# Attention kernel on one core: two value products behind the next block's scores, maxima rows first in each score group, denominators split 3 and 1

## The chip, the cores and the metric

The kernel runs on one core of a Trainium2 chip. The metric is device time in microseconds (us), from the first to the last instruction of one execution. Engines are named as in the profile: PE is TensorE's matmuls, PEld its weight loads, DVE is VectorE, ACT is ScalarE, POOL is GpSimd, SP is SyncE, which issues most transfers.

## The reference, cut to what matters

Sixteen images of 128 channels and 32 x 32 pixels go through a convolution-style attention, then a second, linear attention over tokens, then a mixture of experts. The change touches the first attention alone. It has 4 heads of 32 channels over 1024 pixels, so each image has four 1024 x 1024 score matrices.

```python
qkv = jnp.einsum('oc,bchw->bohw', qkv_w, xn) + qkv_b[:, None, None]
q, k, v = (qkv[:, :, :hd], qkv[:, :, hd:2 * hd], qkv[:, :, 2 * hd:])
attn = jnp.einsum('bnchw,bncyx->bnhwyx', q, k) / jnp.sqrt(jnp.float32(C))
attn = jax.nn.softmax(attn.reshape(B, n, H, W, H * W), axis=-1)
av = jnp.einsum('bnhwyx,bncyx->bnchw', attn, v).reshape(B, C, H, W)
out = jnp.einsum('oc,bchw->bohw', out_w, av) + out_b[:, None, None]
```

## The kernel before, in words

The program is written out per engine and runs as a software pipeline. One iteration belongs to one image for its softmax attention, and holds later stages of the images before it and early stages of the image after it. An iteration is cut into 32 quarters `q`, four to a step: `s, j = divmod(q, 4)`. Every engine walks through the same quarters in its own queue, and semaphores alone tie the queues together.

A block is 128 keys against 512 queries (half an image) for all four heads. An image has 16 blocks, two in each step: their scores stand on PE at j = 0 and j = 2. In what follows a **score group** is the eight products of `scores`: four of q and k, one per head, with 32 rows of contraction each (L1755), then four of the "maxima rows" with 2 rows of contraction in bf16 (L1758). The latter subtract each query's maximum, so that the exponential stays in range. The four heads' products go to four banks of PSUM (the matmul output memory), and the four stand in different row strips of the array, so they run side by side. ACT then takes the exponential of a block in two halves (L928), and PE may write the next score group only when both are done (the wait on `exp_done`). A **values group** is the four products of `values` (L1789) that multiply one block's probabilities with v. They lie side by side in column strips.

The maxima have to be known before the exponential. PE therefore computes the scores of the image or half that comes later a second time with bf16 operands, one **row tile** of 128 queries x 512 keys at a time (L1814), and DVE reduces each to its maxima (L1345). The row tiles alternate between two PSUM banks (`row_ps`). A quarter has two of them, `row_tile(0)` and `row_tile(1)`, and each waits until DVE has read the tile two before it:

```python
ps = row_ps[kh]
pe.wait_ge(row_used, n - 1)
```

Between the two row tiles of a quarter stand the **pieces**: products of the other stages (projections L1602, L1609, L1627; transposes; the rank of tokens L1664 to L1668; the Gram matrix L1639), set to quarters by the table `AT`. Pieces and softmax denominators share one PSUM bank, and `free_shared` waits until it has been drained. The denominators (L1736) sum the probabilities over keys. POOL first adds the blocks of a pair (L729), four pairs to a half, and `DEN_STEPS` says which pairs' products stand in which of two quarters that follow each other.

Of the kernel before, what the change touches and what calls it, by code (L numbers as in the profile page):

```python
# [19 lines left out]
def conv_attention_hybrid_kernel(  # L20
# [25 lines left out]
    NH = 4  # L46
    HD = C // NH
# [4 lines left out]
    E, _, HID = L1_ffn_W1.shape  # L52
# [30 lines left out]
    out_v = out.rearrange("b c h w -> b c (h w)")  # L83


    AT = {'q0': 2, 'k0': 3, 'q1': 4, 'k1': 7, 'rank': 1, 't2_0': 8, 't2_1': 10, 'proj0': 11, 'proj1': 12, 'mrow1': 14, 'v0': 13, 'v1': 16, 'z2T0': 17, 'z2T1': 18, 'logits': 20, 'zT0': 23, 'zT1': 27, 'mrow0': 29, 'gram': 28, 'usum': 30, 'xn': 0, 'values1': 0, 'values0': 17, 'x_bias': 27, 'ln1': 11, 'z2': (12, 14, 14, 15), 'gexp': 21, 'ln0': 16, 'z': (18, 18, 20, 21), 'square': 21, 'ln_heads': 26, 'split': (2, 3, 5, 6), 'norm1': 5, 'norm0': 29, 'd16': (20, 20), 'u': (22, 23), 'scatter': (8, 10, 11, 13, 16, 17, 22, 24), 'max1': 12, 'max0': 28, 'kv1': 2, 'kv2': 4, 'kv3': 5, 'slot_numbers': 4, 'stats1a': 8, 'stats1b': 10, 'deviations1': 11, 'gate': (20, 21, 23, 23, 24, 25, 25, 25, 26, 26, 26, 27, 27, 27, 27, 27), 'prefix': (27, 28, 30), 'stats0a': 11, 'stats0b': 12, 'deviations0': 17, 'gsum': (19, 20), 'ss': (22, 24), 'heads': 26, 'turn': 1, 'den_sum': 2, 'sum': (5, 9, 13, 19), 'den1': 5, 'den0': 21}

    LAG = {
# [16 lines left out]
    def table(pair, p):  # L105

        return AT if 2 * pair + p < B else AFTER[2 * pair + p - B]

# [7 lines left out]
    def in_range(lag, pair, p):  # L116

        return 0 <= 2 * pair + p + lag < (B if lag > -3 else ROUTED)

    def image(lag, pair, p):  # L120

        return 2 * (pair + (p + lag) // 2) + (p + lag) % 2, pair + (p + lag) // 2, (p + lag) % 2
# [8 lines left out]
    def at_quarter(q, pair, p):  # L131

        return [n for n in order(pair, p) if table(pair, p)[n] == q and in_range(LAG[n], pair, p)]
# [6 lines left out]
    def positive(value):  # L140

        return not isinstance(value, int) or value > 0
# [9 lines left out]
    def row_target(r):  # L152

        return (0, 1, r) if r < 4 else (1, 0, r - 4) if r < 8 else (1, 1, 0)

    def denominators_at(pair, p):

        return tuple((table(pair, p)[n], LAG[n], int(n[3])) for n in order(pair, p) if n[:3] == "den")

    DEN_STEPS = ((0, (0, 1)), (1, (2, 3)))  # L160

    def ring_slots(n):

        slots = list(range(NKB))
        for _ in range(n):
            slots = slots[1::2] + slots[0::2]
        return slots
# [7 lines left out]
    def startup_rows(b, half):  # L175

        return b == 0 and half == 0
# [10 lines left out]
    def steps_before(s, n):  # L188

        return (0, s - n) if s >= n else (-1, STEPS + s - n)  # L190
# [38 lines left out]
    with ctx:  # L229
        def sb(name, shape, dt=F32):  # L230
            return ctx.enter_context(nc.sbuf_tensor(name, shape, dt))
# [44 lines left out]
        ones_b = sb("ones_b", [P, P], BF16)  # L276
# [3 lines left out]
        xn = sb("xn", [P, N])  # L280
        part = sb("part", [P, 2, 2, N], BF16)
        qk = sb("qk", [P, 2, 2, N])
# [7 lines left out]
        mrow = sb("mrow", [P, 2, HALF], BF16)  # L290
# [13 lines left out]
        z = sb("z", [P, BLK, C])  # L304
        gsum = sb("gsum", [P, 2, BLK * NG])
        d16 = sb("d16", [P, BLK, C])
        ss16 = sb("ss16", [P, 7, BLK * NG])
        rs16 = sb("rs16", [P, 2, BLK * NG])
        u = sb("u", [P, BLK, C + 1])
        usum = sb("usum_sb", [P, 1])  # L310
# [66 lines left out]
        row_ps, st_ps, av_ps, shared_ps = bank[0:2], bank[2:6], bank[6], bank[7]  # L377
# [1191 lines left out]
        def _(pe):  # L1569
            t_ = nc.tensor  # L1570
# [171 lines left out]
            def scores(b, par, s, j):  # L1742

                half, kb = s // 4, 2 * (s % 4) + j // 2
                keys = slice(kb * P, (kb + 1) * P)
                queries = slice(half * HALF, (half + 1) * HALF)
                if kb == 0:
                    pe.wait_ge(mrow_ready, 2 * b + half + 1)
                    if half == 0:
                        pe.wait_ge(raw_ready, 4 * b + 4)  # L1750
                if positive(32 * b + 4 * s + j):
                    pe.wait_ge(exp_done, 32 * b + 4 * s + j)
                for h in range(NH):
                    rows_ = slice(HD * h, HD * h + HD)
                    t_.matmul(st_ps[h], qk[rows_, par, 1, keys], qk[rows_, par, 0, queries], start=True, stop=False)  # L1755
                for h in range(NH):
                    rows_ = slice(HD * h, HD * h + 2)
                    last = t_.matmul(st_ps[h], ones_b[rows_, :], mrow[rows_, half, :], start=False, stop=True)  # L1758
                    if h % 2 == 1:
                        last.then_inc(st_ready, 1)  # L1760

# [14 lines left out]
            def values(b, par, sv, g):  # L1776

                half = sv // 4
                kb = 2 * (sv % 4) + g
                pe.wait_ge(exp_done, 32 * b + 4 * sv + 2 * g + 2)  # L1780
                if kb == 0:

                    if positive(2 * b + half):
                        pe.wait_ge(av_out, 2 * b + half)
                    pe.wait_ge(v_ready, 2 * b + 2)
                group = prob_groups[ring_slots(2 * b + half)[kb]]
                for h in range(NH):
                    rows_ = slice(HD * h, HD * h + HD)
                    mm = t_.matmul(av_ps[rows_, :], v_sb[:, par, kb, rows_], group[:, h, :],  # L1789
                                   start=(kb == 0), stop=(kb == NKB - 1))  # L1790
                if g == 1:
                    mm.then_inc(probs_used, 1)

            def iteration(pair, p):
                at = table(pair, p)
                for q in range(QUARTERS):
                    s, j = divmod(q, 4)
                    if 2 * pair + p == FIRST and q == OTHER_WEIGHTS_AT:
                        other_weights()

                    def row_tile(kh):
                        lag, half, h = row_target(s + 1)
                        if not in_range(lag, pair, p):
                            return
                        b, pr, par = image(lag, pair, p)
                        if startup_rows(b, half):
                            return
                        if half == (1 if b == 0 else 0) and j == 0 and kh == 0:
                            pe.wait_ge(stacked1[par][h], 16 * STACK1_DMAS * (pr + 1))
                        n = 64 * b + 32 * half + 8 * h + 2 * j + kh  # L1810
                        ps = row_ps[kh]
                        pe.wait_ge(row_used, n - 1)
                        qb = 4 * half + j
                        t_.matmul(ps[:, :], qs1[:, par, h, qb * P:(qb + 1) * P],  # L1814
                                  ks1[:, par, h, kh * HALF:(kh + 1) * HALF], start=True, stop=True)\
                          .then_inc(row_ready, 1)

                    for first, u in FIRST_ROWS:
                        if 2 * pair + p == FIRST and q == first:
                            first_rows(u)  # L1820
                    if j % 2 == 1:
                        lag, sv = (steps_before(s, 1) if j == 1 else (0, s))
                        if in_range(lag, pair, p):
                            b, _, par = image(lag, pair, p)
                            values(b, par, sv, 1 if j == 1 else 0)
                    for first, lag, half in denominators_at(pair, p):
                        for later, pairs in DEN_STEPS:
                            if q == first + later and in_range(lag, pair, p):
                                if later == 0:
                                    free_shared(f"den{half}", pair, p)  # L1830
                                denominators(image(lag, pair, p)[0], half, pairs)
                    if j % 2 == 0 and in_range(0, pair, p):
                        b, _, par = image(0, pair, p)
                        scores(b, par, s, j)
                    row_tile(0)
                    for name in at_quarter(q, pair, p):
                        if name[:3] != "den":
                            piece(name, pair, p)
                    row_tile(1)
                    for t in steps_at(q, pair, p):  # L1840
                        step(t)
# [171 lines left out]
```

## Time and profile before

| what | value |
| --- | --- |
| median of 3 runs | 1842.6 us (1842.03, 1842.6, 1848.09) |
| profiled execution | span 1848.0 us, near the third of these runs |
| PE, PEld | 1707.3 us busy (92%), 842.7 us (46%) |
| DVE, ACT, POOL | 1338.6 us (72%), 1140.8 us (62%), 1279.6 us (69%) |
| softmax stage | from 52.6 us (first exponential) to 1377.6 us (end of the last) |

Read it by stages. The change acts in the softmax stage only, which is 16 iterations long; the experts behind it keep their instructions. In that stage the shares of the engines differ from those of the whole span, so they are taken from a window of their own. PE's busy time includes the overlap of pipelined products, and so the start of one product and the start of the next are read rather than durations.

### The profile page before, as it was taken

To read this page: it belongs to the slowest core of one execution; us is meant where nothing else is said; L and a number is where in the kernel's file an instruction comes from. 1 tells how busy PE (TensorE), PEld (TensorE's weight loads), DVE (VectorE), ACT (ScalarE), POOL (GpSimd) and SP (SyncE) were. 2 spreads that over 40 slices of the span, in tenths; PEclk is the share of its full clock that TensorE was granted. 3 is DMA by queue.
4 is the path that set the end of the run, shared out by engine and by line. 5 is a ranking of instruction groups with operands and counts; after the bars stand their busy time and mean duration, and the time that the engine had idled before them with its cause. 6 is when DMAs were issued, how large, how long until landed. Compare 5 with 4: busy or idle time off the path is not lost. (4 is left out here: it accounts for less than half of the span.)

```text
span 1848.0 us, 36083 instructions
## 1 busy us (share of the span) xinstructions
PE 1707.3 (92%) x11741; PEld 842.7 (46%) x11741; DVE 1338.6 (72%) x3555; ACT 1140.8 (62%) x2019; POOL 1279.6 (69%) x1165
## 2 busy tenths in 40 slices
PE   5999989999999999999999999999976889999999
PEld 2223333333434333333334343333335778888776
DVE  5567788888878888888878888878755555555474
ACT  2556565666656665666666566656544777777553
POOL 1466747787878778787778787787874767777500
PEclk8899999999999999999999999999997889999998
DMA  2302112130303031230303030312212334454394
GB/s 77 91 13 58 35 47 61 46 90 29 88 19 88 19 92 46 65 85 23 92 27 89 19 89 18 92 37 63 67 58 78 92 95 127 156 173 137 102 288 157
DMA packets 119206, 144.43 MB, mean 78 GB/s; under 512 B 18248, under 2 KB 83044, under 8 KB 119024
## 3 DMA queue, kind: packets, MB, share of 16 engines
q1 hardware_dynamic: 103856, 110.91, 21.4%
q0 software_dynamic: 14784, 31.23, 5.0%
q8 instruction: 97, 1.59, 0.4%
q14 instruction: 85, 0.70, 0.1%
q10 hardware_dynamic: 384, 0.00, 0.0%
HBM read 59.38 MB, written 50.05 MB: 59 GB/s over the span
## 5 line engine op out<-in xcount | busy, mean ns | idle before, releaser
L1345 DVE TENSOR_REDUCE rowmax<-psum 128x1 f32<-128x512 f32 x992 | 652.3, 682 | 210.0 <-PE psum L1814 203.9
L1814 PE MATMUL psum<-arena 128*128 128x512 bf16 x992 | 360.4, 390 | 38.2 <-DVE rowmax L1345 35.7
L928 ACT ACTIVATE arena<-psum 128x1024 f32<-128x1024 f32 x256 | 253.9, 1022 | 161.1 <-PE psum L1758 161.1
L928 ACT ACTIVATE probs<-psum 128x1024 f32<-128x1024 f32 x256 | 253.1, 1020 | 114.5 <-PE psum L1758 114.2
L1755 PE MATMUL psum<-qk 32*128 32x512 f32 x2048 | 293.9, 643 | 10.0 <-ACT probs L928 4.6
L1814 PEld LDWEIGHTS psum<-arena 128*128 128x128 bf16 x992 | 88.5, 99 | 448.0 <-DVE rowmax L1345 333.4
L715 POOL DMA_INDIRECT sorted_scratch<-rows,slot_idx x224 | 220.3, 984 | 96.8 <-issue 51.9
L729 POOL TENSOR_TENSOR probs<-probs 128x512 f32<-128x512 f32 x172 | 218.9, 1273 | 27.2 <-PE psum L1789 16.1
L729 POOL TENSOR_TENSOR arena<-arena 128x512 f32<-128x512 f32 x172 | 218.9, 1272 | 22.0 <-PE psum L1789 10.1
L803 POOL DMA_INDIRECT y_scratch<-xn,d_tile x120 | 116.9, 974 | 57.5 <-issue 28.7
L1865 PE MATMUL psum<-qk 128*128 128x256 f32 x476 | 129.5, 396 | 20.0 <-ACT qk L988 18.9
L803 POOL DMA_INDIRECT y_scratch<-qk,d_tile x118 | 115.0, 974 | 45.9 <-issue 26.0
L706 POOL TENSOR_TENSOR part<-qk,part 128x512 bf16<-128x512 f32 x64 | 74.0, 1157 | 94.3 <-ACT qk L848 90.7
L1789 PE MATMUL psum<-arena,v_sb 128*32 128x512 f32 x1024 | 138.5, 613 | 0.0
L1789 PE MATMUL psum<-probs,v_sb 128*32 128x512 f32 x1024 | 136.4, 605 | 0.0
L1755 PEld LDWEIGHTS psum<-qk 32*128 32x128 f32 x2048 | 80.5, 183 | 120.5 <-issue 78.3
L1882 PEld LDWEIGHTS psum<-arena,x_in 128*128 128x128 f32 x952 | 128.0, 198 | 13.8 <-issue 7.5
L1882 PE MATMUL psum<-arena,x_in 128*128 x952 | 130.9, 282 | 3.1 <-ACT x_in L1000 3.1
L1000 ACT ACTIVATE x_in<-psum,b_tile 128x256 f32<-128x256 f32 x238 | 100.0, 472 | 38.4 <-issue 31.8
L729 POOL TENSOR_TENSOR arena<-arena,probs 128x512 f32<-128x512 f32 x80 | 102.1, 1277 | 12.9 <-PE psum L1789 7.6
L729 POOL TENSOR_TENSOR probs<-probs,arena 128x512 f32<-128x512 f32 x80 | 102.0, 1275 | 5.5
L1758 PE MATMUL psum<-mrow,ones_b 2*128 2x512 bf16 x1024 | 102.0, 378 | 0.0
(256 smaller groups left out, 2876.5 us busy)
## 6 DMA issues: line engine op xcount, KB each, us to landing
arena<-part SPq DMA_DIRECT2D x256, 128.0 KB, 3.1
part<-sorted_scratch SPq DMA_DIRECT2D x119, 144.0 KB
x_in<-in_x_dram SPq DMA_DIRECT2D x16, 512.0 KB, 3.2
x_res<-in_x_dram SPq DMA_DIRECT2D x16, 512.0 KB, 5.7
t_scratch<-t SPq DMA_DIRECT2D x14, 512.0 KB, 6.4
arena<-t_scratch SPq DMA_DIRECT2D x10, 512.0 KB
probs<-y_scratch SPq DMA_DIRECT2D x16, 256.0 KB, 4.2
out_dram<-v_sb SPq DMA_DIRECT2D x16, 256.0 KB, 3.9
```

The lines of the kernel that those rows point to most:

```text
L715: g.indirect_dma_start(out=sorted_dram, out_offset=bass.IndirectOffsetOnAxis(ap=slot_idx[:, par, n:n + 1], axis=0), in_=rows[:, par, n % B ...
L729: piece = g.tensor_tensor(even[:, cols], even[:, cols], odd[:, cols], ALU.add)
L803: g.indirect_dma_start(out=y_dram, out_offset=bass.IndirectOffsetOnAxis(ap=d_tile[:, i, k:k + 1], axis=0), in_=y_out[i][:, k, :], in_offse ...
L928: a.activation(group[:, 2 * i:2 * i + 2, :].rearrange("p s n -> p (s n)"), st_pair[i], ACT.Exp, scale=float(C) ** -0.5).then_inc(exp_done, 1)
L1000: a.activation(hid[t % 2][:, j, :], bank[t % 2][:, j * TILE:(j + 1) * TILE], ACT.Gelu, bias=b1_tile[:, t % 2, j:j + 1]).then_inc(hid_ready, 1)
L1345: v.tensor_reduce(rowmax[:, half, kh, h, j:j + 1], row_ps[kh][:, :], AX.X, ALU.max)\
L1755: t_.matmul(st_ps[h], qk[rows_, par, 1, keys], qk[rows_, par, 0, queries], start=True, stop=False)
L1758: last = t_.matmul(st_ps[h], ones_b[rows_, :], mrow[rows_, half, :], start=False, stop=True)
L1789: mm = t_.matmul(av_ps[rows_, :], v_sb[:, par, kb, rows_], group[:, h, :], start=(kb == 0), stop=(kb == NKB - 1))
L1814: t_.matmul(ps[:, :], qs1[:, par, h, qb * P:(qb + 1) * P], ks1[:, par, h, kh * HALF:(kh + 1) * HALF], start=True, stop=True)\
L1865: last = t_.matmul(bank[t % 2][:, j * TILE:(j + 1) * TILE], w1_tile[t % 2][:, j * P:(j + 1) * P], zT_tile[t % 2], start=True, stop=True)
L1882: last = t_.matmul(bank[4 + t % 2][:, k * P:(k + 1) * P], hid[t % 2][:, j, k * P:(k + 1) * P], w2[:, bass.ds(e, 1), j, :].rearrange("p a c ...
```

## The change

Three things are done. The two values groups of a step, which stood at j = 1 and j = 3 (each between the row tiles of two quarters), now both stand at j = 0 straight behind the score group, and they take the two blocks of the step before. In a score group the maxima rows go first and open the accumulation, and the products of q and k close it, so that the semaphore for ACT now hangs on these. The denominators' pairs go three and one instead of two and two, and stand behind the scores of their quarter. ACT's evacuation of the values of the first half moves one quarter up (`values0`).

```diff
-'values0': 17
+'values0': 16
...
-    DEN_STEPS = ((0, (0, 1)), (1, (2, 3)))
+    DEN_STEPS = ((0, (0, 1, 2)), (1, (3,)))
...
                 for h in range(NH):
+                    rows_ = slice(HD * h, HD * h + 2)
+                    t_.matmul(st_ps[h], ones_b[rows_, :], mrow[rows_, half, :], start=True, stop=False)
+                for h in range(NH):
                     rows_ = slice(HD * h, HD * h + HD)
-                    t_.matmul(st_ps[h], qk[rows_, par, 1, keys], qk[rows_, par, 0, queries], start=True, stop=False)
-                for h in range(NH):
-                    rows_ = slice(HD * h, HD * h + 2)
-                    last = t_.matmul(st_ps[h], ones_b[rows_, :], mrow[rows_, half, :], start=False, stop=True)
+                    last = t_.matmul(st_ps[h], qk[rows_, par, 1, keys], qk[rows_, par, 0, queries], start=False, stop=True)
                     if h % 2 == 1:
                         last.then_inc(st_ready, 1)
...
-                    if j % 2 == 1:
-                        lag, sv = (steps_before(s, 1) if j == 1 else (0, s))
+                    if j % 2 == 0 and in_range(0, pair, p):
+                        b, _, par = image(0, pair, p)
+                        scores(b, par, s, j)
+                    if j == 0:
+                        lag, sv = steps_before(s, 1)
                         if in_range(lag, pair, p):
                             b, _, par = image(lag, pair, p)
-                            values(b, par, sv, 1 if j == 1 else 0)
+                            values(b, par, sv, 0)
+                            values(b, par, sv, 1)
...
-                    if j % 2 == 0 and in_range(0, pair, p):
-                        b, _, par = image(0, pair, p)
-                        scores(b, par, s, j)
```

The next two fences show PE's order in the first step of an iteration, from the score group at q = 0 on: L1755 and L1758 are the score group, L1814 the row tiles, L1789 the values, L1664 to L1668 the rank. First before:

```order
L1755 MATMUL psum<-qk 128x512 x4
L1758 MATMUL psum<-mrow,ones_b 128x512 x4
L1814 MATMUL psum<-arena 128x512 x2
L1789 MATMUL psum<-arena,v_sb 32x512 x4
L1814 MATMUL psum<-arena 128x512
L1664 MATMUL psum<-chosen,tri 128x64
L1666 MATMUL psum<-before,ones 128x64
L1668 MATMUL psum<-before,ones 128x8
L1814 MATMUL psum<-arena 128x512
```

And in the changed kernel, at the same place:

```order
L1755 MATMUL psum<-mrow,ones_b 128x512 x4
L1758 MATMUL psum<-qk 128x512 x4
L1789 MATMUL psum<-probs,v_sb 32x512 x4
L1789 MATMUL psum<-arena,v_sb 32x512 x4
L1814 MATMUL psum<-arena 128x512 x3
L1664 MATMUL psum<-chosen,tri 128x64
L1666 MATMUL psum<-before,ones 128x64
L1668 MATMUL psum<-before,ones 128x8
L1814 MATMUL psum<-arena 128x512
```

Two values groups now stand ahead of the first row tile of the step, and between the step's row tiles none is left; the line numbers 1755 and 1758 have changed their products. The second place is the denominators of an image's second half, at q = 5 and 6 of the following iteration; L1602 is the projection to q that stands at q = 4, L1736 the denominators. Before, again on PE:

```order
L1755 MATMUL psum<-qk 128x512 x4
L1758 MATMUL psum<-mrow,ones_b 128x512 x4
L1814 MATMUL psum<-arena 128x512
L1602 MATMUL psum<-xn,wqkvT 128x512
L1814 MATMUL psum<-arena 128x512
L1789 MATMUL psum<-probs,v_sb 32x512 x4
L1736 MATMUL psum<-probs,ones 32x512 x8
L1814 MATMUL psum<-arena 128x512 x2
L1736 MATMUL psum<-probs,ones 32x512 x8
L1755 MATMUL psum<-qk 128x512 x4
```

And changed:

```order
L1755 MATMUL psum<-mrow,ones_b 128x512 x4
L1758 MATMUL psum<-qk 128x512 x4
L1789 MATMUL psum<-arena,v_sb 32x512 x8
L1814 MATMUL psum<-arena 128x512
L1602 MATMUL psum<-xn,wqkvT 128x512
L1814 MATMUL psum<-arena 128x512
L1736 MATMUL psum<-probs,ones 32x512 x12
L1814 MATMUL psum<-arena 128x512 x2
L1755 MATMUL psum<-mrow,ones_b 128x512 x4
L1758 MATMUL psum<-qk 128x512 x4
L1736 MATMUL psum<-probs,ones 32x512 x4
```

The values group that stood between L1602 and the first denominators has gone ahead of L1602, three pairs stand together, and the fourth comes behind the next score group. On DVE and SP nothing moves; on ACT the evacuation L911 goes ahead of two small operations.

## Rows read from the trace of the kernel before

**Rows 1.** Busy time of each engine in the softmax stage (count of instructions in brackets).

```profile
52.60:1377.60 1325.00, 1252.76 (x8954) 477.40 (x8953) 1051.82 (x2443) 836.24 (x1252) 1016.59 (x863) 0.98 0.20 57
```

**Rows 2.** Groups of instructions: busy us, mean ns; idle time before them, what ended it.

```profile
L1345 DVE TENSOR_REDUCE rowmax<-psum 128x1 f32<-128x512 f32 x992 | 652.3, 682 | 210.0 <-PE psum L1814 203.9
L1814 PE MATMUL psum<-arena 128*128 128x512 bf16 x992 | 360.4, 390 | 38.2 <-DVE rowmax L1345 35.7
```

**Rows 3.** Timeline of PE, first step of an image: start, duration (us), instruction.

```profile
622.46 1.14 PE L1755 MATMUL psum<-qk 32*128 32x512 f32 x8
623.42 0.40 PE L1758 MATMUL psum<-mrow,ones_b 2*128 2x512 bf16 x4
623.75 0.64 PE L1814 MATMUL psum<-arena 128*128 128x512 bf16 x2
624.32 1.07 PE L1789 MATMUL psum<-probs,v_sb 128*32 128x512 f32 x8
625.32 0.39 PE L1814 MATMUL psum<-arena 128*128 128x512 bf16 x1
...
626.13 0.38 PE L1814 MATMUL psum<-arena 128*128 128x512 bf16 x1
626.44 1.14 PE L1755 MATMUL psum<-qk 32*128 32x512 f32 x8
...
627.73 0.39 PE L1814 MATMUL psum<-arena 128*128 128x512 bf16 x1
...
631.67 1.14 PE L1755 MATMUL psum<-qk 32*128 32x512 f32 x8
```

**Rows 4.** Timeline of PE, second step of the same image, with the denominators.

```profile
633.19 1.02 PE L1602 MATMUL psum<-xn,wqkvT 128*128 128x512 f32 x2
...
635.56 1.06 PE L1736 MATMUL psum<-arena,ones 128*32 128x512 f32 x8
...
637.42 0.60 PE L1814 MATMUL psum<-arena 128*128 128x512 bf16 x2
...
639.81 1.14 PE L1755 MATMUL psum<-qk 32*128 32x512 f32 x8
...
642.63 0.39 PE L1814 MATMUL psum<-arena 128*128 128x512 bf16 x1
642.99 1.10 PE L1602 MATMUL psum<-xn,wqkvT 128*128 128x512 f32 x2
643.92 0.38 PE L1814 MATMUL psum<-arena 128*128 128x512 bf16 x1
644.23 1.14 PE L1755 MATMUL psum<-qk 32*128 32x512 f32 x8
```

**Rows 5.** Timeline of DVE in that first step.

```profile
624.18 1.29 DVE L1345 TENSOR_REDUCE rowmax<-psum 128x1 f32<-128x512 f32 x2 [0.23 <-PE psum L1814]
```

**Rows 6.** Timeline of all engines in a later step: a row tile that waits.

```profile
770.34 0.39 PE L1814 MATMUL psum<-arena 128*128 128x512 bf16 x1
...
770.60 0.65 DVE L1345 TENSOR_REDUCE rowmax<-psum 128x1 f32<-128x512 f32 x1
...
771.31 0.39 PE L1814 MATMUL psum<-arena 128*128 128x512 bf16 x1 [0.58 <-DVE rowmax L1345]
```

**Rows 7.** Timeline of ACT in the first and second step.

```profile
627.89 1.02 ACT L928 ACTIVATE probs<-psum 128x1024 f32<-128x1024 f32 x1 [0.43 <-PE psum L1758]
629.02 0.69 ACT L846 ACTIVATE part<-psum,bqk 128x512 bf16<-128x512 f32 x1
...
630.17 1.02 ACT L928 ACTIVATE probs<-psum 128x1024 f32<-128x1024 f32 x1
...
634.25 0.69 ACT L846 ACTIVATE part<-psum,bqk 128x512 bf16<-128x512 f32 x1
634.83 0.68 ACT L848 ACTIVATE qk<-psum,bqk 128x512 f32<-128x512 f32 x1
```

**Rows 8.** Group of the Gram products, in the same columns as rows 2.

```profile
L1639 PE MATMUL psum<-u 128*128 128x129 f32 x256 | 47.4, 361 | 20.3 <-POOL u L787 20.3
```

More of the change, by code:

```diff
@@ L83, in conv_attention_hybrid_kernel @@
     out_v = out.rearrange("b c h w -> b c (h w)")
-    AT = {'q0': 2, 'k0': 3, 'q1': 4, 'k1': 7, 'rank': 1, 't2_0': 8, 't2_1': 10, 'proj0': 11, 'proj1': 12, 'mrow1': 14, 'v0': 13, 'v1': 16, 'z2T0': 17, 'z2T1': 18, 'logits': 20, 'zT0': 23, 'zT1': 27, 'mrow0': 29, 'gram': 28, 'usum': 30, 'xn': 0, 'values1': 0, 'values0': 17, 'x_bias': 27, 'ln1': 11, 'z2': (12, 14, 14, 15), 'gexp': 21, 'ln0': 16, 'z': (18, 18, 20, 21), 'square': 21, 'ln_heads': 26, 'split': (2, 3, 5, 6), 'norm1': 5, 'norm0': 29, 'd16': (20, 20), 'u': (22, 23), 'scatter': (8, 10, 11, 13, 16, 17, 22, 24), 'max1': 12, 'max0': 28, 'kv1': 2, 'kv2': 4, 'kv3': 5, 'slot_numbers': 4, 'stats1a': 8, 'stats1b': 10, 'deviations1': 11, 'gate': (20, 21, 23, 23, 24, 25, 25, 25, 26, 26, 26, 27, 27, 27, 27, 27), 'prefix': (27, 28, 30), 'stats0a': 11, 'stats0b': 12, 'deviations0': 17, 'gsum': (19, 20), 'ss': (22, 24), 'heads': 26, 'turn': 1, 'den_sum': 2, 'sum': (5, 9, 13, 19), 'den1': 5, 'den0': 21}
+    AT = {'q0': 2, 'k0': 3, 'q1': 4, 'k1': 7, 'rank': 1, 't2_0': 8, 't2_1': 10, 'proj0': 11, 'proj1': 12, 'mrow1': 14, 'v0': 13, 'v1': 16, 'z2T0': 17, 'z2T1': 18, 'logits': 20, 'zT0': 23, 'zT1': 27, 'mrow0': 29, 'gram': 28, 'usum': 30, 'xn': 0, 'values1': 0, 'values0': 16, 'x_bias': 27, 'ln1': 11, 'z2': (12, 14, 14, 15), 'gexp': 21, 'ln0': 16, 'z': (18, 18, 20, 21), 'square': 21, 'ln_heads': 26, 'split': (2, 3, 5, 6), 'norm1': 5, 'norm0': 29, 'd16': (20, 20), 'u': (22, 23), 'scatter': (8, 10, 11, 13, 16, 17, 22, 24), 'max1': 12, 'max0': 28, 'kv1': 2, 'kv2': 4, 'kv3': 5, 'slot_numbers': 4, 'stats1a': 8, 'stats1b': 10, 'deviations1': 11, 'gate': (20, 21, 23, 23, 24, 25, 25, 25, 26, 26, 26, 27, 27, 27, 27, 27), 'prefix': (27, 28, 30), 'stats0a': 11, 'stats0b': 12, 'deviations0': 17, 'gsum': (19, 20), 'ss': (22, 24), 'heads': 26, 'turn': 1, 'den_sum': 2, 'sum': (5, 9, 13, 19), 'den1': 5, 'den0': 21}
     LAG = {
```

## The prediction

> **What bounds the kernel now.** I read the windows by stage first. In the softmax stage (1325 us of the 1848.0) PE is busy 1252.76 us, 95%, DVE 1051.82 (79%), POOL 77% and ACT 63% [rows 1]. So PE looks like the bound. The groups of instructions then show with whom it is interlocked: the 992 row tiles of PE and the 992 maxima of DVE are the pair with the most waiting between them. DVE waits 203.9 us for row tiles, PE itself only 35.7 us for maxima [rows 2]. Third I read the timeline of one image, to see how these waits are kept small: in the step of [rows 3] no two row tiles start more than 1.60 us apart (626.13 and 627.73), and two of them last DVE 1.29 [rows 5].
>
> The timeline gives every price needed, as the distance from one start to the next [rows 3]. A score group lasts 0.96 to its maxima rows and 0.33 from there to the next row tile: 1.29. A values group lasts 625.32 - 624.32 = 1.00. From a row tile to a group in strips it is 626.44 - 626.13 = 0.31; from a row tile to the next it is 0.22 (two last 0.60, one 0.38) [rows 4]. Hence each entry into strips costs 0.09. A step without pieces is 2 x (1.29 + 1.00 + 2 x 0.22 + 2 x 0.31) = 6.70 us of PE; the mean of 128 steps (16 images of 8) is 1325 / 128 = 10.35, and the other 3.65 are pieces, denominators and waits.
>
> **The change, part by part.**
>
> *Maxima rows first.* The same eight products. The two passes of a score product then end the group. A values group has the same two passes and exit, 1.00, and a pass of 512 columns is 0.22, so I take 1.22 for the group. Bounds: 1.29 (nothing gained), and 1.08 if it also loses its exit as the second of two groups in strips does (0.86 + 0.22). Gain 0.07 per group.
>
> *Two values groups together.* Two pairs of denominators, products of the same shape, last 637.42 - 635.56 = 1.86 [rows 4], so the second group adds 0.86 rather than 1.00. The entry falls away twice in a step. PE saves 2 x 0.07 + 0.14 + 2 x 0.09 = 0.46 us a step.
>
> *What the values groups leave behind.* A row tile may start only when DVE has read the tile two before it. DVE starts a maximum 0.43 us after its tile (623.75 and 624.18), takes 0.68, and follows with the next after 1.29 - 0.68 = 0.61 [rows 2, 3, 5]; the waiting tile starts 0.06 after the maximum's end (771.31 against 770.60 + 0.65) [rows 6]. So behind an idle DVE the third tile comes no sooner than 0.43 + 0.68 + 0.06 = 1.17 after the first, and the fourth 0.61 later. Before, a values group (0.31 + 1.00) lies exactly between the second and third tile and hides this. Afterwards it stands ahead of the first tile, where DVE has its two last tiles to read (1.29) and PE brings nothing for 1.22 + 1.86 + 0.31 = 3.39.
>
> The first step, worked from its score group at 0 [rows 3]. Values to 3.08, first tile there; DVE 3.51 to 4.19; third tile 4.25; the rank between third and fourth takes 626.13 - 625.32 = 0.81, fourth tile 5.06; next score group 5.37. Before it was 626.44 - 622.46 = 3.98: 1.39 longer. The second half of the step loses its values group, but the next score group needs the exponentials. ACT ends the second at 630.17 + 1.02 = 631.19, which is 4.75 after the score group, with two copies of a projection between the two exponentials [rows 7]. This chain shortens by the 0.07 only, and a release takes 0.05, so the half lasts 4.73 against 631.67 - 626.44 = 5.23: 0.50 shorter. The step is 0.89 longer. With no piece and no exponential in the way the halves would be 5.17 and 3.31, 1.78 more than 6.70; with full cover by pieces the step would be 0.46 shorter. I take 0.87 for the five steps of this kind (first, third, fourth, fifth, seventh), by the one that I worked.
>
> *Denominators 3 and 1.* Their count stays. In the second step the first of them wait for ACT's two copies of L1602's projection: they start at 635.56, 0.05 after 634.83 + 0.68 [rows 4, 7], which is 2.37 behind L1602. Afterwards L1602 starts at 3.30 (values, tile, 0.22), the denominators at 5.67; three pairs 1.86 + 0.86, two tiles 0.53, next scores at 8.92. Before: 639.81 - 631.67 = 8.14. In the second half: scores and one pair to 2.22, third tile 3.39, then 644.23 - 642.63 = 1.60 as before: 4.99 against 4.42. The step is 1.35 longer. In the sixth step another piece stands there; without its wait the step would be 1.13 shorter than that, +0.2; I take 0.5. POOL's sums are asked for no sooner in the last pair, which stays a quarter behind; its cover is the two row tiles and the score group ahead of it.
>
> *The Gram step.* In the eighth step PE waits for POOL ahead of the Gram products, 20.3 us over 16 images [rows 8]. The second values group in front hides in this 1.27, the second half is shorter by 0.50 as above: -0.5.
>
> *Free.* The evacuation of values a quarter earlier on ACT follows exponentials that end later than the values do; if that cover is gone it delays ACT by at most the values' 1.86 once in an image. That PE asks POOL for sums sooner costs nothing while POOL has 23% idle.
>
> Sum per image: 5 x 0.87 + 1.35 + 0.5 - 0.5 = 5.7. Fifteen images have the row tiles of a following one throughout (the last I count at nothing): 85 us. Against the profiled 1848.0 that is 1933; that execution lies 5.4 over the median, so 1928.
>
> **The rivals.** *PE is the bound and simply has less to do* (faster). 128 x 0.46 = 59: 1784. For it: PE's 95%, and that PE's waits for DVE are so few. Against it: they are few because something always stands between the tiles. It decides if the waits at the third tile and for exponentials come to less than 0.46 us a step, that is if pieces stand there in most steps.
> The skill speaks for this rival: the Trainium skill, "TensorEngine Tiling (Array Packing)", Key Properties, says that changing the tiling mode drains TensorE. The trace agrees, with the 0.09 at each entry; by that rule alone the time would be the 1784 above.
>
> *Exponentials alone hold it.* DVE's waits are covered by pieces, and only the second halves cannot shrink below ACT's chain. First halves grow by 0.86 - 0.07 - 0.09 = 0.70, second ones fall by 0.50: 0.20 a step, 120 steps: 24, so 1867. For it: rows 7 hold in any case. Against: in the step worked, DVE's term is the larger.
>
> *It cancels* (no change). DVE's other work is about (1051.82 - 652.3) / 15 = 27 us an image; if half of it moves into the new gaps, tiles behind it come sooner, and the 5.7 goes to nothing: 1843. Against: DVE's queue is in order, and jobs that stand behind a maximum cannot go ahead of it.
>
> **How the numbers follow.** Forecast 1928: 0.66. Exponentials alone, 1867: 0.13. No change: 0.08. Faster: 0.13. For the forecast's own bounds: score groups at 1.29 add 16 x 0.07 x 15 = 17, at 1.08 they take 34; the four plain steps not worked may come to +0.20 (-40 us) or +1.78 (+55). Not all at once: 1875 to 1965 for the likeliest case. The range reaches down to the exponentials' case and a little under, 1850 to 1965. Within 0.3% (5.5 us) is about what a measurement of this kernel cannot tell from no change; slower then has 0.79.
>
> **What would show it.** After the change: row tiles' starts with "DVE rowmax" as releaser and several times the 35.7 us on PE; DVE's wait for L1814 well over 203.9; first halves of a step near 5.4 us, second ones 3.3 to 4.7; PE's share in the stage falling to about 85 to 90% with fewer us of busy time. A score group of 1.22 and values at 1.86 would confirm the savings. The prediction is wrong if third tiles start 0.22 behind the second, or if the PE saving shows in the image's length.

## The result: 6.1% slower, and the profile after

The changed kernel takes 1958.45 us (median of 4 runs, 1955.56 to 1959.46) against 1843.64 for the kernel before: a ratio of 1.0607, 95% interval 1.0583 to 1.0631. The forecast was 1928, range 1850 to 1965, slower with 0.79. Direction and the main part of the mechanism held; the size was 85 us where 115 were measured (108 between the two profiled executions, 1956.2 against 1848.0).

First the windows view of the softmax stage after, which answers to [rows 1] (length, busy us of PE, PEld, DVE, ACT, POOL, clock):

```profile
52.60:1488.00 1435.40, 1230.93 (x8962) 480.36 (x8960) 1021.44 (x2444) 834.74 (x1252) 1017.71 (x863) 0.99 0.19 52
```

PE is busy 1230.93 us of 1435.40, 86% instead of 95%, and does its work in 21.83 us less. So the work did shrink; the stage grew by waits. Which waits, the groups show beside [rows 2]:

```profile
L1345 DVE TENSOR_REDUCE rowmax<-psum 128x1 f32<-128x512 f32 x992 | 645.0, 680 | 324.2 <-PE psum L1814 318.0
L1814 PE MATMUL psum<-arena 128*128 128x512 bf16 x992 | 355.8, 389 | 111.9 <-DVE rowmax L1345 107.9
```

PE's idle time for maxima went from 35.7 to 107.9 us, and DVE's for row tiles from 203.9 to 318.0. Each waits more for the other and neither has become the busier one, as is to be expected where a hand-over has lost its cover. The list of PE's waits after (what waited, for whom: us in total, times, longest) names the rest:

```profile
PE psum L1814 <- DVE rowmax L1345: 107.9, 236, 1.8
...
PE psum L1736 <- ACT qk L848: 16.0, 14, 1.1
PE psum L1602 <- ACT qk L848: 13.5, 15, 1.0
PE psum L1755 <- ACT probs L928: 13.4, 18, 2.3
PE psum L1755 <- ACT arena L928: 11.4, 19, 2.0
PE psum L1639 <- POOL u L787: 8.2, 15, 1.1
...
PE psum L1626 <- DVE t L1214: 7.1, 15, 0.9
...
PE psum L1634 <- DVE rden L1122: 5.4, 15, 0.9
...
PE psum L1602 <- DVE rden L1122: 4.5, 14, 0.3
PE psum L1659 <- ACT v_sb L853: 4.5, 13, 0.3
PE psum L1609 <- ACT t L861: 3.6, 14, 0.3
...
PE psum L1616 <- ACT kvw L866: 2.1, 12, 0.2
```

Read by kind. Maxima: +72.2. Pieces and denominators that wait until ACT or DVE has drained the shared PSUM bank (L1736, L1602, L1626, L1634, L1659, L1609, L1616): 56.7 in these rows, against 1.2 in the same list of before (L1626 0.9, L1609 0.3). Score groups for exponentials: 24.8 against 8.9. The Gram products for POOL: 8.2 against 20.3, a gain of 12.1. PE's busy time over the whole span falls by 1707.3 - 1683.7 = 23.6. Together 72.2 + 55.5 + 15.9 - 12.1 - 23.6 = 107.9, and the spans differ by 108.2. (The rows of the two lists that are left out here nearly cancel; they come to -0.2.) This says where PE stands, not yet why: the experiments have to show that.

The first step of an image on PE after the change, beside [rows 3]:

```profile
678.63 0.40 PE L1755 MATMUL psum<-mrow,ones_b 2*128 2x512 bf16 x4
...
681.68 0.60 PE L1814 MATMUL psum<-arena 128*128 128x512 bf16 x2
682.85 0.39 PE L1814 MATMUL psum<-arena 128*128 128x512 bf16 x1 [0.57 <-DVE rowmax L1345]
...
683.97 0.39 PE L1755 MATMUL psum<-mrow,ones_b 2*128 2x512 bf16 x4
...
687.86 1.10 PE L1602 MATMUL psum<-xn,wqkvT 128*128 128x512 f32 x2 [0.84 <-ACT qk L848]
...
689.10 0.39 PE L1755 MATMUL psum<-mrow,ones_b 2*128 2x512 bf16 x4
```

The values end at 681.68, 3.05 after the scores' start; the third row tile comes 1.17 behind the first; the half lasts 5.34 (forecast 5.37). The second half lasts 5.13 (forecast 4.73): its last piece, the projection to k, finds the shared bank still occupied by the projection to q, and stands 0.84 us until ACT has copied it (687.86). The values group that stood between the two had hidden this.

### The profile page after: what moved, and what is told of

The parts are those of the page before. It is cut to its first block and busy times, and to the rows that moved or that the text cites. A ratio compares the mean times of both kernels' runs of the same rounds, so it can differ in the third digit from the quotient of the medians.

```text
span 1956.2 us, 36083 instructions
## 1 busy us (share of the span) xinstructions
PE 1683.7 (86%) x11741; PEld 844.4 (43%) x11741; DVE 1306.6 (67%) x3555; ACT 1138.9 (58%) x2019; POOL 1280.8 (65%) x1165
## 3 DMA queue, kind: packets, MB, share of 16 engines
q1 hardware_dynamic: 103856, 110.91, 20.4%
## 5 line engine op out<-in xcount | busy, mean ns | idle before, releaser
L1345 DVE TENSOR_REDUCE rowmax<-psum 128x1 f32<-128x512 f32 x992 | 645.0, 680 | 324.2 <-PE psum L1814 318.0
L1814 PE MATMUL psum<-arena 128*128 128x512 bf16 x992 | 355.8, 389 | 111.9 <-DVE rowmax L1345 107.9
L1814 PEld LDWEIGHTS psum<-arena 128*128 128x128 bf16 x992 | 89.7, 99 | 467.0 <-DVE rowmax L1345 314.1
L1758 PE MATMUL psum<-qk 32*128 32x512 f32 x2048 | 268.6, 597 | 0.0
L1789 PE MATMUL psum<-probs,v_sb 128*32 128x512 f32 x1024 | 132.2, 621 | 0.0
L1789 PE MATMUL psum<-arena,v_sb 128*32 128x512 f32 x1024 | 127.1, 600 | 0.0
L1755 PE MATMUL psum<-mrow,ones_b 2*128 2x512 bf16 x1024 | 102.0, 388 | 26.8 <-ACT probs L928 13.4
L1000 ACT ACTIVATE x_in<-psum,b_tile 128x256 f32<-128x256 f32 x238 | 99.8, 471 | 38.9 <-issue 32.3
L1758 PEld LDWEIGHTS psum<-qk 32*128 32x128 f32 x2048 | 103.8, 188 | 4.1
```

What stands on the lines that cost most here:

```text
L1000: a.activation(hid[t % 2][:, j, :], bank[t % 2][:, j * TILE:(j + 1) * TILE], ACT.Gelu, bias=b1_tile[:, t % 2, j:j + 1]).then_inc(hid_ready, 1)
L1345: v.tensor_reduce(rowmax[:, half, kh, h, j:j + 1], row_ps[kh][:, :], AX.X, ALU.max)\
L1758: last = t_.matmul(st_ps[h], qk[rows_, par, 1, keys], qk[rows_, par, 0, queries], start=False, stop=True)
L1814: t_.matmul(ps[:, :], qs1[:, par, h, qb * P:(qb + 1) * P], ks1[:, par, h, kh * HALF:(kh + 1) * HALF], start=True, stop=True)\
```

## The experiments

Seven kernels follow from the change or the kernel before by one or two edits each; two more reduce the row tiles in both. Ratios are to the kernel before, measured beside each group of runs (medians 1848.75, 1847.64 and 1843.98). The traces of these nine lack records of row tiles (839 to 841 of 992 are there, 361 and 374 of 496 in the last two; before and after lack none), so their waits for maxima are less exact. Where a step's length is given below, it is read from the starts of the score groups, of which no trace lacks one. The kernel with denominators 2 and 2, as long as the change, lists 114.0 us of them where the change has 107.9: differences of some 6 us say nothing there.

**The maxima rows first, alone.** The kernel before with this edit:

```diff
-    t_.matmul(st_ps[h], qk[...], qk[...], start=True, stop=False)
...
-    last = t_.matmul(st_ps[h], ones_b[...], mrow[...], start=False, stop=True)
+    t_.matmul(st_ps[h], ones_b[...], mrow[...], start=True, stop=False)
...
+    last = t_.matmul(st_ps[h], qk[...], qk[...], start=False, stop=True)
```

> Only the score groups are reordered (maxima rows first); values and denominators stay where they were before. Tile hand-over theory (the loss comes from taking the values groups from between the row tiles): a score group lasts 1.19 instead of 1.29, so 256 of them save up to 27 us, part of it eaten by waits: 1815 to 1835, faster than 1843.6. Rival, the score order itself delays the exponentials: slower than before, part of the 115 us. Rival, no effect because TensorE is not the bound: within 0.3% of 1843.6.

Measured: 1840.38 us, ratio 0.9957 (0.994 to 0.9973). Faster by 8 us, 0.4%, where 9 to 29 were expected (1815 to 1835 against 1843.6). The timeline of PE in this kernel shows the group's new length:

```profile
645.07 0.39 PE L1755 MATMUL psum<-mrow,ones_b 2*128 2x512 bf16 x4
645.30 1.03 PE L1758 MATMUL psum<-qk 32*128 32x512 f32 x8
```

The maxima rows take 0.23 ahead of the products of q and k, and the products 0.96 (in the changed kernel 70.01 to 70.97, below): 1.19 instead of 1.29. The saving is real, 256 x 0.10 = 26 us; some two thirds of it turn into waits. The largest new one is 16 us at the Gram products, whose wait for POOL is 36.6 us here against 20.3 in [rows 8]. This part does not make the loss; alone, it is the one version with all of the work in it that is faster than both kernels.

**The pair of values groups, alone.** Old score groups, and denominators 2 and 2; the values as in the change, and with them its order within a quarter (scores ahead of denominators) and `values0` at 16:

```diff
-    last = t_.matmul(st_ps[h], qk[...], qk[...], start=False, stop=True)
+    last = t_.matmul(st_ps[h], ones_b[...], mrow[...], start=False, stop=True)
...
-    DEN_STEPS = ((0, (0, 1, 2)), (1, (3,)))
+    DEN_STEPS = ((0, (0, 1)), (1, (2, 3)))
```

> Only the two values groups stand together behind the scores (with the order of the quarter that this needs and the evacuation at 16); score groups in the old order, denominators 2 and 2. Tile hand-over theory: as slow as the change or slower, by up to 256 x 0.10 = 27 us: 1955 to 1985. Rival, the score order or the denominators make the loss: within 1% of 1843.6. The row tiles' waits for maxima on TensorE stay above 90 us by the first, near 36 by the second.

Measured: 1978.55 us, ratio 1.0702 (1.0686 to 1.0717). All of the loss is in this part: 130 us. The maxima-first order gives some of it back, for the split of the denominators, the only other difference to the change, is free (next experiment). What moving the scores ahead of the denominators costs by itself was not tested. PE's waits for maxima in this kernel:

```profile
PE psum L1814 <- DVE rowmax L1345: 108.4, 226, 1.8
```

**Denominators 2 and 2 in the change.**

```diff
-    DEN_STEPS = ((0, (0, 1, 2)), (1, (3,)))
+    DEN_STEPS = ((0, (0, 1)), (1, (2, 3)))
```

> The whole change, but denominators 2 and 2. Tile hand-over theory: the same work in the same two quarters, 1950 to 1966, same as the change. Rival, three pairs together delay the following score group: 10 us or more faster than the change.

Measured: 1957.34 us, ratio 1.0584 (1.0569 to 1.0599). The interval overlaps the change's own: the split makes no difference that these runs can tell.

**The pair between row tiles.** The change, with the pair one place later in the step (and `values0` in the table of slots from 16 to 17):

```diff
-                    if j == 0:
+                    if j == 1:
                         lag, sv = steps_before(s, 1)
```

> The whole change, but the pair of values groups stands one quarter later, at j = 1, between the second and the third row tile of the first half; evacuation back at 17. Tile hand-over theory: the pair again covers the hand-over in first halves, which fall from about 5.4 to 4.2 us in a step without pieces; second halves stay uncovered. So roughly half of the loss comes back or more: 1870 to 1915. Rival, the exponentials and the copies on ScalarE hold the second halves, or TensorE's order of strips matters: no better than the change, 1945 to 1965.

Measured: 1921.88 us, ratio 1.0388 (1.0373 to 1.0403). Some 40 us come back, between the two expectations: clearly better than the change, short of the half that the hand-over theory promised. In the first image's step without pieces, the first half lasts 4.12 (68.37 to 72.48) where the change has 5.14 (below): there the pair covers the hand-over as expected. PE still waits 92.7 us for maxima in all:

```profile
PE psum L1814 <- DVE rowmax L1345: 92.7, 182, 2.8
```

One step takes back much of the gain. In the median of twelve images from the fourth on, the second to the seventh step are together 4.2 us shorter than in the change, but the eighth, with the Gram products, is 2.5 longer. It has lost the pair that had covered it: PE waits 20.4 us there for POOL against 8.2 in the change, which is some 0.8 of the 2.5; the rest was not followed up. The mean granted clock from 100 to 1300 us was 0.97 here against 0.99 in the change, so a part of what is missing may be clock.

**One values group behind each score group.** The change, unpaired:

```diff
-                    if j == 0:
-                        lag, sv = steps_before(s, 1)
+                    if j % 2 == 0:
+                        lag, sv = (steps_before(s, 1) if j == 0 else (0, s))
                         if in_range(lag, pair, p):
                             b, _, par = image(lag, pair, p)
-                            values(b, par, sv, 0)
-                            values(b, par, sv, 1)
+                            values(b, par, sv, 1 if j == 0 else 0)
```

> The changed kernel, but one values group directly behind each of the two score groups of a step (j = 0 and j = 2) instead of two behind the first; maxima first and denominators 3 and 1 as in the change. Nothing is paired, but no values group stands between row tiles either. Tile hand-over theory: a half without pieces lasts 1.19 + 1.00 + 0.43 + 0.61 + 0.68 + 0.06 + 0.31 = 4.28, two of them 8.56 against the change's 8.42: as slow as the change, 1940 to 1975. Rival, the pairing itself makes the loss (the second halves without a cover for exponentials and copies): near the kernel before, 1835 to 1870.

Measured: 1959.19 us, ratio 1.0604 (1.058 to 1.0628): the change to 0.1%. So pairing is not what costs; the place is. Behind a score group, with no row tile between, the values cost the same one by one or in a pair.

**Half of each maximum left out**, in the kernel before and in the change. DVE reads 256 of the 512 columns:

```diff
-    v.tensor_reduce(rowmax[...], row_ps[kh][:, :], AX.X, ALU.max)
+    v.tensor_reduce(rowmax[...], row_ps[kh][:, 0:HALF // 2], AX.X, ALU.max)
```

> The kernel before, with VectorE reducing only the first 256 of the 512 columns of each row tile (it leaves out half of the maxima). A maximum should fall from 0.68 us to about 0.4. Tile hand-over theory: before, the hand-over is mostly covered, so that only part of the 36 us of waits for maxima on TensorE goes: 1810 to 1840. Rival, VectorE's sum of work is the bound of the stage: 992 x 0.27 = 270 us less work, well under 1780.

> The changed kernel, with the same halved maxima (it leaves out half of the maxima). Tile hand-over theory: the third tile comes 0.27 us sooner behind the first, the fourth again 0.27 sooner, about 0.5 us in each of 256 half steps where nothing else holds: 60 to 110 us back of the 115, so 1850 to 1900, and the waits for maxima on TensorE fall from 108 us to under 40. Rival, exponentials and copies on ScalarE hold the second halves, whatever VectorE takes: 1930 to 1958.

Measured: 1813.57 us before (ratio 0.9816, 0.9791 to 0.984) and 1914.62 in the change (1.0373, 1.0348 to 1.0397). The first is as expected: DVE's maxima fall from 652.3 to 396.0 us, by 256, and the kernel loses 34, so DVE's sum is no bound. The second is a miss for both theories: 43 us come back, not 60 to 110, and the gap between the pair stays at 101. The groups and waits of the halved change:

```profile
L1345 DVE TENSOR_REDUCE rowmax<-psum 128x1 f32<-128x256 f32 x992 | 393.2, 416 | 484.7 <-remote 245.0 <-PE psum L1814 237.5 <-issue 0.5
```

```profile
PE psum L1814 <- DVE rowmax L1345: 53.0, 133, 1.5
PE psum L1755 <- ACT probs L928: 27.2, 32, 2.3
PE psum L1755 <- ACT arena L928: 24.6, 35, 2.0
...
PE psum L1736 <- ACT qk L848: 16.0, 14, 1.1
```

A maximum fell only from 0.68 to 0.42, and the 0.43 + 0.06 of the hand-over's two ends do not shrink with it. The first image's step without pieces shows what this leaves:

```profile
70.88 0.61 PE L1814 MATMUL psum<-arena 128*128 128x512 bf16 x2
71.79 0.72 PE L1814 MATMUL psum<-arena 128*128 128x512 bf16 x2 [0.30 <-DVE rowmax L1345]
72.44 0.40 PE L1755 MATMUL psum<-mrow,ones_b 2*128 2x512 bf16 x4
...
75.73 0.39 PE L1755 MATMUL psum<-mrow,ones_b 2*128 2x512 bf16 x4 [0.47 <-ACT probs L928]
```

The third tile comes 0.91 behind the first (1.18 in the change, below), and the first half, which starts at 67.84, falls from 5.14 to 4.60. The second half stays at 3.29 (72.44 to 75.73): the next score group now waits for exponentials. In such a half, maxima and exponentials hold PE equally long in the change, and shortening the maxima alone gains nothing. Waits for maxima about halve (107.9 to 53.0), those for exponentials double (24.8 to 51.8), and those for the shared bank hardly move (16.0 and 13.5 at the two longest of them, 16.0 and 12.9 here). The hand-over of row tiles is then not the only wait that the values groups covered.

**One row tile per quarter**, again in both kernels. To see what is left without the hand-over, each quarter computes and reads one row tile (the second half of the keys is left out of the maxima), and the two banks go in turn:

```diff
-                        if not in_range(lag, pair, p):
+                        if kh == 1 or not in_range(lag, pair, p):
                             return
...
-                        ps = row_ps[kh]
-                        pe.wait_ge(row_used, n - 1)
+                        ps = row_ps[n // 2 % 2]
+                        pe.wait_ge(row_used, 32 if n == 32 else n - 2)
```

> The kernel before with one row tile per quarter instead of two, the two PSUM banks in turn (it leaves out the second half of the keys from the maxima). A half step then has two row tiles and two banks for them, so no tile needs the bank of a tile of its own half. 496 tiles of 0.23 us fall away on TensorE, 114 us, of which waits for exponentials and for the shared bank take some back: 1740 to 1800.

> The changed kernel with the same single row tile per quarter (it leaves out the same maxima). Hand-over of row tiles alone: nothing is left to wait for, TensorE has about 0.5 us a step less to do, so it is faster than the run before this one, by 20 to 60 us. Hand-over plus drains of the shared bank and exponentials (about 76 us of TensorE's new waits in the changed kernel's list, against 72 us for maxima): the waits for maxima fall under 10 us, the drains stay, and it remains slower than the run before this one, by 10 to 60 us.

Measured: 1820.37 us (ratio 0.9853, 0.9817 to 0.989) and 1882.88 (1.0192, 1.0162 to 1.0222). The first misses its range by 20: 496 tiles less on PE bring only 24 us, because other waits take their place: 58.3 us for exponentials (8.9 before), 37.9 at the Gram products (20.3), and 28.9 at the denominators for POOL's sums (3.2):

```profile
PE psum L1639 <- POOL u L787: 37.9, 15, 2.8
PE psum L1755 <- ACT arena L928: 30.4, 56, 1.5
PE psum L1755 <- ACT probs L928: 27.9, 50, 1.3
```

The mean granted clock was lower too, 0.96 from 52.6 to 1350 us against 0.98 in [rows 1]; what that costs was not separated. In the second of the pair it was 0.97, so the clock does not make the gap between the two. The second remains slower than the first by 62.5, a little over the upper end of what hand-over plus drains expected (10 to 60); the hand-over alone is refuted. Its waits:

```profile
PE psum L1755 <- ACT arena L928: 50.8, 45, 2.1
PE psum L1755 <- ACT probs L928: 41.4, 44, 2.3
PE psum L1814 <- DVE rowmax L1345: 25.6, 27, 1.4
PE psum L1634 <- DVE rden L1122: 19.8, 15, 1.4
...
PE psum L1736 <- ACT qk L848: 19.0, 14, 1.4
PE psum L1602 <- DVE rden L1122: 18.9, 14, 1.4
...
PE psum L1602 <- ACT qk L848: 18.5, 15, 1.2
```

Row tiles wait for maxima 25.6 us, not under 10 as expected: DVE's other jobs still stand ahead of some maxima (L1170 with 1.98 us ends ahead of the one at 1285.13). Yet the shared bank and the exponentials hold PE most. By this pair some 62 of the 115 us stay without the second row tile of each quarter, 25.6 of PE's waits in it still being for maxima, and about 52 go with it. The shares are measured in a thinner kernel, whose first member has new waits of its own, and so they are no exact split of the change itself.

## Why the prediction was right, point by point

*The savings on PE.* A score group is 1.19 (forecast 1.22). Two values groups last 1.85 (72.82 - 70.97 in the rows below; forecast 1.86). The entry into strips falls away as forecast. Both durations held to 0.03 us.

*The hand-over.* The first image has a step with no pieces at all, and there the formula can be read off PE's timeline after the change:

```profile
69.78 0.39 PE L1755 MATMUL psum<-mrow,ones_b 2*128 2x512 bf16 x4
70.01 1.03 PE L1758 MATMUL psum<-qk 32*128 32x512 f32 x8
70.97 1.92 PE L1789 MATMUL psum<-arena,v_sb 128*32 128x512 f32 x16
72.82 0.60 PE L1814 MATMUL psum<-arena 128*128 128x512 bf16 x2
74.00 0.39 PE L1814 MATMUL psum<-arena 128*128 128x512 bf16 x1 [0.57 <-DVE rowmax L1345]
74.59 0.39 PE L1814 MATMUL psum<-arena 128*128 128x512 bf16 x1 [0.21 <-DVE rowmax L1345]
74.92 0.39 PE L1755 MATMUL psum<-mrow,ones_b 2*128 2x512 bf16 x4
...
78.21 0.40 PE L1755 MATMUL psum<-mrow,ones_b 2*128 2x512 bf16 x4
```

Third tile 1.18 behind the first, fourth 0.59 later, halves of 5.14 and 3.29 where 5.17 and 3.31 were forecast for a step without pieces. The first half bears the formula out. The second does not decide: ACT's exponentials there end at 76.21 + 1.94 = 78.15, only 0.06 before the next score group at 78.21, so they alone would give the same 3.29, and with halved maxima they do.

*The first step.* 5.34 + 5.13 = 10.47 against the forecast 10.10 and 9.21 before. First half right. In the second half the wait was put on the exponentials alone; PE's row at 687.86 shows that it was the shared bank.

*Denominators.* The waiting chain through ACT was right, and so was the first half of the second step:

```profile
694.75 1.06 PE L1736 MATMUL psum<-arena,ones 128*32 128x512 f32 x8 [1.14 <-ACT qk L848]
...
698.00 0.40 PE L1755 MATMUL psum<-mrow,ones_b 2*128 2x512 bf16 x4
...
702.07 1.10 PE L1602 MATMUL psum<-xn,wqkvT 128*128 128x512 f32 x2 [0.32 <-DVE rden L1122]
...
703.31 0.40 PE L1755 MATMUL psum<-mrow,ones_b 2*128 2x512 bf16 x4
```

From 689.10 to 698.00 it is 8.90 (forecast 8.92); the second half is 5.31 (forecast 4.99). The 0.32 between them is the wait at 702.07, again for the shared bank, which DVE has first to clear of the denominators. That this part stays the same whether the pairs stand 3 and 1 or 2 and 2, its experiment shows.

*The sum.* Twelve images from the fourth on, read at their first score groups, after:

```profile
317.39 0.39 PE L1755 MATMUL psum<-mrow,ones_b 2*128 2x512 bf16 x4
...
1400.65 0.40 PE L1755 MATMUL psum<-mrow,ones_b 2*128 2x512 bf16 x4
```

and before:

```profile
285.39 1.14 PE L1755 MATMUL psum<-qk 32*128 32x512 f32 x8
...
1298.22 1.14 PE L1755 MATMUL psum<-qk 32*128 32x512 f32 x8
```

An image takes (1400.65 - 317.39) / 12 = 90.27 us against (1298.22 - 285.39) / 12 = 84.40: 5.87 more, where the sum said 5.7. The term of the sum that was mis-sized is the last one, which counts fifteen images at 5.7 and the last at nothing. The first three images, before the pipeline is full of pieces, grew, from the first score group of all (start 49.77 after, 50.03 before), by (317.39 - 49.77) - (285.39 - 50.03) = 32.3 us, nearly 11 each, for 17 in the sum. What follows the start of the last image came to (1956.2 - 1400.65) - (1848.0 - 1298.22) = 5.8 us more, for 0; 5.3 of them lie between its first and its last score group. These 21.0 us and 12 x 0.17 = 2.0, less the 0.3 by which the first score group starts sooner, are the difference between 85.5 and 108.2. For the first three images the rows above give a reason: with few pieces a step pays nearly the whole 1.78 that was worked out (the step without pieces takes 8.43 after, 78.21 - 69.78, and 6.76 before). PE's list of waits, cut to these three images, has 29.4 us for maxima after and 7.9 before, two thirds of the 32.3. The rest was not followed up; the granted clock differs there as well (0.50, the lower of its two levels, from 50 to 61 us before; 0.55 in the mean from 124.5 to 136 after).

*A right sum of two half-right parts.* That 5.87 came so near 5.7 is partly luck. In the mean of the same twelve images the eight steps grew by 1.22, 1.65, 1.19, 0.64, 1.16, 0.45, 0.84 and -1.29 us. The five that were put at 0.87 each, by the one that was worked, came to 5.05 instead of 4.35, and the second to 1.65 instead of 1.35; the sixth was right (0.5). The Gram step, put at -0.5, gained 0.79 more than that, and so hid the other errors. As to causes, the prediction attributed the loss to row tiles, to exponentials in second halves and to one wait at the denominators. The list of waits gives maxima 72.2 us but drains of the shared bank 55.5, of which the prediction had only the 16.0 at L1736; and it put exponentials as the limit of second halves where in the worked step the shared bank was.

*The rivals.* "PE is the bound and has less to do" is refuted: PE does have 23.6 us less to do and the kernel is 115 slower. The Trainium skill, "TensorEngine Tiling (Array Packing)", Key Properties, says that changing the tiling mode drains TensorE. The trace agrees, with 0.09 us at an entry. Of the 0.46 us a step behind this rival's 1784, 0.14 comes from the order within the score groups, which that rule does not bear on. "Exponentials alone" had the right place for part of the waits (24.8 us after, 8.9 before), but its waits grew by 15.9 us of 108, and the halved maxima bring 43 us back in the change, which it excludes. "It cancels" is refuted by the result.

## What to carry to other kernels

An engine that is 95% busy is not therefore the one to relieve: ask of each product on it what would be waited for if it stood elsewhere. Here the values groups were the filler between two row tiles that share banks with VectorE and between pieces that share one PSUM bank, and the change that moved them cost 115 us while PE's busy time fell by 24 (the move alone cost 130). Before grouping like products to save switches, price a switch (0.09 us here) against the shortest hand-over that the group now covers no longer (1.17 us here), per occurrence.

## What the runs showed of the hardware that was not expected

The order within a group of products in four row strips matters: with the 2-row bf16 products ahead of the two-pass f32 products the group takes 0.23 + 0.96 = 1.19 us, with them behind it 0.96 + 0.33 = 1.29, for the same eight products.

A maximum over half of the columns is far from half as long: 0.416 us for 256 columns against 0.680 for 512.
